# A bound on the row numbers of a gather: edge scores of a graph network that leave out lanes outside the step's block

## What is computed

```python
enh = x + 0.1 * query_emb
Q, K, V = enh @ Wq + bq, enh @ Wk + bk, enh @ Wv + bv
scores = einsum('ehd,ehd->eh', Q[dst], K[src] + 0.2 * rel_w[edge_type]) / 8
w = softmax of scores over the edges of one dst
agg = segment_sum(w * V[src], dst)
...
x = layernorm(x + layer0);  x = layernorm(x + layer1)
```

## Time and profile before

| what | value |
|---|---|
| median of 3 runs | 6380.61 us (6377.07 to 6381.08) |
| the profiled execution | 6381.05 us |
| its span, first to last instruction | 6379.2 us |
| busy: PE, DVE, POOL, ACT | 68%, 69%, 68%, 41% of the span |
| DMA: moved in all, mean rate | 1362.40 MB, 214 GB/s |
| queue q0 (DMAs that POOL issues) | 644.62 MB, 35.8% of the 16 engines' span |
| queue q1 (DMAs that SP issues) | 597.85 MB, 28.3% |
| gathers of the scores, line 709 | 1664, of 128 rows each |

### The profile page before, as it was taken

One profiled execution on the slowest core, in us unless ns is written; L12 is line 12 of the kernel. 1 busy time (PEld: TensorE's weight loads), 2 busy tenths in 40 slices (PEclk: granted clock), 3 DMA queues, 4 the chain that ended last, 5 costly groups with the idle time before them and its releaser, 6 DMA issues. The chain is left out here.

```text
span 6379.2 us, 69851 instructions
## 1 busy us (share of the span) xinstructions
PE 4348.0 (68%) x14703; PEld 2925.8 (46%) x14703; DVE 4423.7 (69%) x9217; ACT 2622.2 (41%) x6438; POOL 4317.9 (68%) x4007
## 2 busy tenths in 40 slices
PE   9856666665566665554999997995666666666662
PEld 5544444444444444443666664443334333333331
DVE  8857777777777775668888887994555555555557
ACT  2133333333333333334888884772222222222223
POOL 0057777777777776744888884557777777777773
PEclk9977777777777777776999998997777877777776
DMA  7678888888888888863777773336666666666664
GB/s 232 203 234 285 280 283 282 283 282 282 284 281 281 283 283 284 280 204 115 247 246 247 247 245 91 102 90 167 163 162 161 162 161 162 161 162 162 161 162 141
DMA packets 785385, 1362.40 MB, mean 214 GB/s; under 512 B 91415, under 2 KB 455607, under 8 KB 784653
## 3 DMA queue, kind: packets, MB, share of 16 engines
q0 software_dynamic: 208288, 644.62, 35.8%
q1 hardware_dynamic: 509773, 597.85, 28.3%
q10 hardware_dynamic: 66914, 115.46, 5.9%
HBM read 1059.09 MB, written 298.50 MB: 213 GB/s over the span
## 5 line engine op out<-in xcount | busy, mean ns | idle before, releaser
L1513 POOL DMA_INDIRECT t_rows<-xj_rows,other x1564 | 1496.2, 957 | 492.5 <-issue 475.5
L1615 PE MATMUL ps_xsum<-t_rows,t_att 128*128 x3328 | 1247.0, 528 | 729.2 <-DVE t_att L1568 728.6
L1615 PEld LDWEIGHTS ps_xsum<-t_rows,t_att 128*128 128x128 f32 x3328 | 751.1, 253 | 1225.5 <-issue 924.2
L1568 DVE SCALAR_TENSOR_TENSOR t_att<-iota,local,t_att 128x128 f32<-128x128 f32 x1664 | 576.0, 347 | 952.2 <-ACT t_att L1547 949.9
L709 POOL DMA_INDIRECT s_rows<-kv_rows,other x832 | 906.0, 1089 | 419.2 <-issue 225.0
L840 PE MATMUL ps_q<-node_tab,hot 128*128 x3328 | 1164.4, 514 | 0.0
L1547 ACT ACTIVATE t_att<-t_att,t_rows 128x128 f32<-128x128 f32 x1664 | 531.2, 389 | 1431.9 <-SPq L1500 1419.4
L834 PE MATMUL ps_small<-rel,hot 128*128 128x128 f32 x1664 | 399.3, 379 | 975.5 <-ACT hot L727 975.4
L709 POOL DMA_INDIRECT s_rows<-vk_rows,other x832 | 878.2, 1056 | 267.8 <-issue 260.8
L723 ACT ACTIVATE apart<-spread,minus_p 128x768 uint8<-128x768 uint8 x416 | 388.8, 935 | 1542.9 <-DMA spread<-what_rows 1542.9
L806 DVE TENSOR_TENSOR s_rows<-s_rows,rel 128x1024 f32<-128x1024 f32 x416 | 510.2, 1226 | 687.5 <-ACT rel L739 687.3
(11 more groups left out here) (227 smaller groups left out, 4070.0 us busy)
## 6 DMA issues: line engine op xcount, KB each, us to landing
v_edges<-s_rows SPq DMA_DIRECT2D x416, 512.0 KB, 14.4
a_terms<-v_edges SPq DMA_DIRECT2D x416, 512.0 KB, 4.8
t_att<-a_rows ACTq DMA_DIRECT2D x416, 256.0 KB, 3.5
spread<-what_rows SPq DMA_DIRECT2D x416, 96.0 KB
t_rows<-xj_rows,other POOLq DMA_INDIRECT x1564, 3.3
kv_rows<-kv_out SPq DMA_DIRECT2D x97, 256.0 KB, 2.1
vk_rows<-kv_out SPq DMA_DIRECT2D x194, 128.0 KB, 2.1
s_rows<-kv_rows,other POOLq DMA_INDIRECT x832, 5.0
```

Of the source, the lines that this page charges most:

```text
L1513: pool.indirect_dma_start(out=rows[:, at:at + XW], out_offset=None, in_=t["xj_rows"], in_offset=bass.IndirectOffsetOnAxis(ap=t["other1"][: ...
L1568: dve.scalar_tensor_tensor(w, t["iota"][:, :], t["local1"][:, g * U + k:g * U + k + 1], w, ALU.is_equal, ALU.mult)\
L1615: nc.tensor.matmul(ps_sum[g % 4][:, k, :], att[g % ATT_RING][:, k, :], xj[k], start=True, stop=True)\
```

## The change

In `build_steps` of layer 0, DVE makes a second array `off_block`: 16,384 where `local` is below 0, and where it is above 127, with partition 0 set to zero, and adds it to `other0`. It does so between nodes_set and the making of `odd`, one instruction after the other. A lane outside its step's block thereby has a row number of at least 16,384. In `edge_scores`, each gather carries a bound of 16,383 and skips rows beyond it without an error, so such a lane keeps what its buffer held. Therefore POOL fills the five buffers with zeros before the first gather and waits for that. Partition 0 always gathers its row. The number of gathers, groups and steps stays.

```diff
+OUTSIDE = 1 << 14
...
+        off_block = None if layer else sb("off_block", [P, S])
...
                 step(dve.tensor_scalar(what[:, 0, :], local[:, :], -1.0, float(P), ALU.max, ALU.min))
                 dve.sem_inc(nodes_set, 1)
+                for edge, beyond in ((0.0, ALU.is_lt), (P - 0.5, ALU.is_gt)):
+                    step(dve.tensor_scalar(off_block[:, :], what[:, 0, :], edge, float(OUTSIDE), beyond, ALU.mult))
+                    step(dve.memset(off_block[0:1, :], 0.0))
+                    step(dve.tensor_tensor(other[:, :], other[:, :], off_block[:, :], ALU.add))
                 step(dve.tensor_copy(odd_bits[:, :], partition[:, 0:1]))
...
+        rows_cleared = sem("s_rows_cleared")
...
+            for r in rows:
+                nc.gpsimd.memset(r[:, :, :], 0.0).then_inc(rows_cleared, 1)
+            pool.wait_ge(rows_cleared, KV_RING)
             for g in range(G):
...
                     pool.indirect_dma_start(out=rows[g % KV_RING][:, k, :], out_offset=None, in_=t["vk_rows"] if k % 2 else t["kv_rows"],
-                                            in_offset=bass.IndirectOffsetOnAxis(ap=t["other0"][:, g * U + k:g * U + k + 1], axis=0))\
+                                            in_offset=bass.IndirectOffsetOnAxis(ap=t["other0"][:, g * U + k:g * U + k + 1], axis=0),
+                                            bounds_check=OUTSIDE - 1, oob_is_err=False)\
                         .then_inc(rows_in[g % KV_RING], 16)
```

More of the change, by code:

```diff
@@ L57 @@
 EPS = 1e-5
+OUTSIDE = 1 << 14
 LOWEST = -1.0e30
-assert PIECE == U * DH and PIECE * PIECES == F and S % P == 0 and C * P >= T and PAD_NODE >= N and PAD_NODE < (1 << NODE_BITS) and NB <= P
+assert N <= OUTSIDE and PIECE == U * DH and PIECE * PIECES == F and S % P == 0 and C * P >= T and PAD_NODE >= N and PAD_NODE < (1 << NODE_BITS) and NB <= P
 def plan_merges():
```

## The result

The kernel after takes **6467.9 us** (median; 6455.4 to 6487.5) against 6379.2 for the kernel before on the same chip: a ratio of 1.0142 [1.0115, 1.0168] (the brackets are the 95% interval), so slower by 1.4%, where 6306 was forecast. Its profiled execution took 6471.87 us, 90.8 more than that of before. Lines of the kernel after lie about ten lower in the code: the gathers are L719, the add L817, product and sum L822 and L824, the long sort pieces L800 and L802, the store of v_edges L698.

A forecast was written before the change was run, and what follows sets the result against it. DMA was taken to bound the score stage, with POOL next: 6381.05 - 88.5 (rows left out) + 4.1 (DVE operations) + 9.4 (POOL clears) = 6306 us. The 8-in-10 range was 6290 to 6425 us.

The forecast's parts named there:

- POOL has 0.225 us of slack per gather: Score stage: a gather takes 1.485 us, but 1.26 left alone; 0.225 us goes to buffer waits and long gathers.
- The price of the bound: Gathers at L709: comparing 128 row numbers adds zero to 0.17 us on POOL per gather, hidden behind DMA.
- rival 1: L709: the comparison makes POOL bound the score stage; slower, 6423 us at 0.242 us per gather, 6713 at 0.416; chance 0.22.
- point of decision: Comparison price per gather at L709 from which the whole change turns slower: 0.22 us.
- Two signs of being right: Score stage: L709's usual duration stays below 1.13 us, and q0 moves 25 MB less.
- The rule on branching: Gathers on POOL: the skill's 12 cycles per element would add 1.28 us per gather, near 8150 us in all.
- Rows left out: Score stage gathers: 12,192 rows of 2 KB, 24.97 MB, save 88.5 us at 282 GB/s (83 to 95).
- the forecast's own mechanism: Score stage stays bound by DMA: the time of the rows left out is saved, the later start is paid in full.
- The start: Before the first gather: six DVE operations delay the stage 4.1 us, POOL's five clears and wait add 9.4 us.
- Rival 2: Score stage: rows go but not the time, or they don't go; only the two starts stay, 6395 us; chance 0.09.
- The range: Whole kernel: 6290 to 6425 us for 8 in 10, holding forecast, rivals and rival 1 up to 0.242 us.

The follow-up runs named there:

- the two psum_rel kernels: The kernel before and the kernel after, each with DVE's add reading the relation rows from PSUM instead of ACT's SBUF copy: 6374.6 and 6324.5 us.
- after_sort_later: Kernel after, with a DVE memset of 128x100 ahead of each sort piece, which waits for the memset's semaphore: 6328.3 us.
- after_psum_rel: Kernel after, with DVE's add reading the relation rows straight from PSUM and ACT's copy gone: 6324.5 us.
- before_psum_rel: Kernel before, without the bound, with DVE's add reading the relation rows straight from PSUM and ACT's copy gone: 6374.6 us.
- after_sort_late: Kernel after, with a DVE memset of 128x100 ahead of each sort piece, without a wait for it: 6486.9 us.
- before_sort_late: Kernel before, with four DVE fills of 128x28 ahead of each sort piece and a small tile added behind minus_p: 6475.7 us (one run).

## Why the prediction was wrong

**The step that failed is "POOL has 0.225 us of slack per gather, spent in waits for a free buffer and in gathers that last up to 2.0 us".** The second half of that sentence was no slack. Of the 2470.7 us, 1664 x 1.262 = 2100 are POOL's own pace (0.957 and a gap of 0.305), 188 are gathers held up by DVE, and only the other 183, 0.11 us per gather, are waits. The maximum of 2017 ns stood in the earlier trace rows beside a median of 957, and the gathers of half as long rows in another stage had a mean of 957; I counted the long gathers as slack and did not look which DVE operation ran beside them.

**After, POOL's sum is full**: 1664 x 1.314 = 2186.5, lengthened 358, waits 6, in all 2550. POOL's work rose by 257 us (87 for the bound's longer pace, 170 for gathers held up); 177 of it went into the former waits, and 80 lengthened the stage. With 13 at its start that makes 93, against 90.8 between the two profiled executions.

**The price of the bound**, the term I called least sure, was in the range taken (0 to 0.17): 0.053 us. By itself it would have just fitted, as 183 - 88.5 leaves 0.057 us per gather. What it did besides, moving the gathers across the start of the sort's pieces, stood in no step. So rival 1 named the right place and the right waits, POOL as the bound at L709 with SP waiting for rows, but by the price of the comparison alone. Its point of decision (0.22 us) held the same false slack: by the real waits it is (183 - 13.5) / 1664 = 0.10, still twice the price measured. By these sums the price alone would not have made the kernel slower; the 170 us of gathers held up besides did. Two signs of being right came true all the same, the usual gather below 1.13 us and 25 MB less on q0; the span of the gathers (2550 for 2382) and SP's waits told the difference.

The rule on branching of the Trainium skill, GPSIMD Engine Reference, section 3.1 Elementwise, is not borne out for the gather's comparison: 0.053 us, where its figure gave 1.28.

**Rows left out: 61 us, not 88.5.** The count was nearly right: 25.18 MB fewer, 12,319 rows and not 12,192. That is 97 x 127: the block end that falls on a tile's edge has a step of its own too (T + NB - 1 = 1660 of the 1664 steps are in use). The time was counted at a DMA rate that stays, but where DMA is the bound again (the two psum_rel kernels) the rate is 279 GB/s where it was 283, and 61 us came of it; after_sort_later, too, spans 60.5 us less than before. A group with a block end needs 4 x 1.314 = 5.26 us on POOL, not 5.04, so DMA's saving may be cut short there. The trace of after_psum_rel bears this out in part: POOL's time for the group behind such a group falls to 5.53 us in the mean (5.91 in before_psum_rel), and half of these take under 5.3 us, where of all groups a third do; that of the fifth group behind falls to 5.62 (5.93). How much of the missing 27 us this explains stays open. With 61 us the forecast's own mechanism gives 6381 - 61 + 13.5 = 6333, near after_sort_later's 6328.

**The start: right.** The timeline of the kernel after, which answers to the earlier trace rows:

```profile
334.37 1.03 DVE L593 TENSOR_SCALAR off_block<-what 128x1664 f32<-128x1664 bf16 x1 [0.16 <-DVE what L590]
...
335.79 1.45 DVE L594 MEMSET off_block<- 1x1664 f32 x1 [0.40 <-DVE off_block L593]
337.27 1.89 DVE L595 TENSOR_TENSOR other<-other,off_block 128x1664 int32<-128x1664 int32 x1
...
344.41 0.15 DVE L598 TENSOR_SCALAR odd<-odd_bits 128x1 f32<-128x1 int32 x1
...
350.79 0.20 POOL L707 MEMSET hot<- 128x128 f32 x1 [59.65 <-POOLq L433]
...
351.02 8.79 POOL L712 MEMSET s_rows<- 128x2048 f32 x5
...
360.70 1.18 POOL L719 DMA_INDIRECT s_rows<-kv_rows,other  x1 [0.90 <-POOL s_rows L712]
```

odd is ready at 344.56 (344.6 forecast). POOL's first clear of the stage starts at 350.79, 4.1 us later than before (346.65), as forecast; the five clears take 8.79 us and add 9.1 with the wait (9.4 forecast). So the first gather starts 13.2 us later (13.5). Rival 2 fell: where POOL has room, most of the rows' time does go. The range, 6290 to 6425, missed the 6468 because its upper end priced rival 1 by a longer comparison (0.242 us) and by no gathers held up.

## What to carry to other kernels

Before counting an engine's long instructions as slack, split them: set the timelines of two engines side by side and ask what the other one ran when the long ones began. An operation that holds up another engine can be moved, delayed or given an operand in PSUM: here that was worth 122 to 143 us, and 25 MB of transfers 61. A few hundredths of a microsecond per instruction can shift two engines that step in a fixed phase, so price a longer instruction by the phase as well as by the sum.

## What was not expected of the hardware

- A gather of 128 rows that starts within a DVE tensor_tensor on two SBUF operands is held until its end, by up to 1.07 us (after_sort_late; 1.06 before); one that started ahead of it, by the records, mostly is not (none of 131 in before, 0.03 us ahead; but 171 in after_sort_late). Product and sum, with PSUM or one operand, hold none.
- A lane beyond the bound stays on the queue: q0 has 208,288 packets in the whole execution before and after, and with half the lanes left out a usual gather still takes 1.009 us on POOL.
- Where the four spread tiles began 32 bytes behind a multiple of 128 bytes per partition (64 in before_sort_late), the rate fell from 282 to 271 GB/s and the time rose by about 100 us. They take the 96 KB loads alone, 768 bytes per partition. Row buffers 96 bytes behind a multiple of 128 lose nothing. Why one transfer pays and the other doesn't stays open.
